# A transformer block's attention groups with their steps written in another order

## The reference

```python
x = L0_attn_u
xn = _layernorm(x, axis=-1)
x = x + _L0_attn_ref(xn, ...) + _L0_ffn_ref(xn, ...)      # state-space convolution; gated FFN
xn = _layernorm(x, axis=-1)
x = x + _L1_attn_ref(xn, ...) + _L1_ffn_ref(xn, ...)      # attention; base + gated low-rank experts
```

```python
H, DN, DV, DQ, HID = 32, 128, 128, 192, 512
q = jnp.einsum('bsd,de->bse', hidden_states, wq).reshape(B, S, H, DQ)
k, v = ...                                                # from wkv, heads of 128
scores = jnp.einsum('bqhd,bkhd->bhqk', q[..., :DN], k) * scale
scores = jnp.where(causal[None, None], scores, NEG_INF)
probs = jax.nn.softmax(scores, axis=-1)
attn = jnp.einsum('bhqk,bkhd->bqhd', probs, v).reshape(B, S, H * DV)
return jnp.einsum('bse,ed->bsd', attn, wo)
```

## Time and profile before

| | |
|---|---|
| Median of 3 runs (lowest, highest) | 1063.7 us (1060.49, 1066.61) |
| The profiled execution: its own time | 1062.6 us |
| Its span, first to last instruction | 1060.7 us |
| Granted TensorE clock | 1.000 of full speed over the whole span |
| Layer 0, up to the first step of group 0 | 0 to 263 us |
| Group 0, groups 1 to 6, group 7 | 263 to 353, 353 to 960, 960 to 1061 us |
| Busy: PE, ACT, SP's DMAs | 1047.7, 543.0, 31.5% of 16 engines |

### The profile page before, as it was taken

One profiled execution on the slowest core, in us unless ns is written; L12 is line 12 of the kernel. 1 busy time (PEld: TensorE's weight loads), 2 busy tenths in 40 slices (PEclk: granted clock), 3 DMA queues, 4 the chain that ended last, 5 costly groups with the idle time before them and its releaser, 6 DMA issues. The chain is left out here.

```text
span 1060.7 us, 19733 instructions
## 1 busy us (share of the span) xinstructions
PE 1047.7 (99%) x6025; PEld 918.1 (87%) x6025; DVE 808.9 (76%) x1959; ACT 543.0 (51%) x1573; POOL 754.8 (71%) x1030
## 2 busy tenths in 40 slices
PE   9999999999999999999999999999999999999998
PEld 8888878898898898878988898889888888888987
DVE  7598974467688687877888787878788778778775
ACT  4454321033764555556555555555556555555663
POOL 4777568897957875977597668848774876587920
PEclk9999999999999999999999999999999999999999
DMA  5111242110232333334333423342434333333412
GB/s 168 51 49 52 97 143 70 60 46 21 76 99 82 115 115 99 98 102 132 80 97 118 133 82 96 104 135 75 126 86 123 87 113 111 105 92 109 119 55 79
DMA packets 108120, 100.67 MB, mean 95 GB/s; under 512 B 72688, under 2 KB 88240, under 8 KB 107888
## 3 DMA queue, kind: packets, MB, share of 16 engines
q1 hardware_dynamic: 107728, 98.89, 31.5%
q10 hardware_dynamic: 288, 0.52, 0.1%
HBM read 74.26 MB, written 25.10 MB: 94 GB/s over the span
## 5 line engine op out<-in xcount | busy, mean ns | idle before, releaser
L2063 ACT ACTIVATE prob<-prob,top 128x128 f32<-128x128 f32 (+1 forms) x256 | 114.2, 448 | 85.2 <-DVE top L2096 84.6
L1724 POOL TENSOR_TENSOR form_lo<-wqk_stage,form_hi 128x256 fp32r<-128x256 f32 x192 | 143.5, 748 | 16.0
L2069 ACT ACTIVATE prob<-prob,inv 128x128 f32<-128x128 f32 (+1 forms) x256 | 102.8, 450 | 51.1 <-DVE inv L2102 51.1
L1778 POOL TENSOR_SCALAR vf_hi<-wvo_stage 128x512 fp32r<-128x512 f32 (+1 forms) x48 | 26.6, 554 | 117.4 <-PE banks L200 85.2
L198 PE MATMUL banks<-tT_hi,form_hi 128*128 128x512 f32 x256 | 103.7, 405 | 0.8 <-DVE qT_lo L1851 0.5
L199 PE MATMUL banks<-tT_lo,form_hi 128*128 128x512 f32 x256 | 100.0, 391 | 0.0
L200 PE MATMUL banks<-tT_hi,form_lo 128*128 128x512 f32 x256 | 100.0, 391 | 0.0
L2096 DVE CUSTOM_DVE_ANT_0 prob<-banks,mask 128x128 f32<-128x128 f32 (+1 forms) x256 | 81.0, 353 | 23.0 <-issue 7.6
L2114 DVE TENSOR_TENSOR acc<-acc,banks 128x512 f32<-128x512 f32 x129 | 86.4, 675 | 15.5 <-PE banks L200 14.3
L198 PE MATMUL banks<-wo_hi,oT_hi 128*128 128x512 f32 x240 | 97.1, 404 | 0.7 <-DVE oT_lo L2133 0.7
L199 PE MATMUL banks<-wo_lo,oT_hi 128*128 128x512 f32 x240 | 93.8, 391 | 0.0
(11 more groups left out here) (358 smaller groups left out, 3638.9 us busy)
## 6 DMA issues: line engine op xcount, KB each, us to landing
bounce<-probT SPq DMA_DIRECT2D x117, 192.0 KB, 1.9
pT<-bounce SPq DMA_DIRECT2D x468, 48.0 KB, 1.9
wqk_stage<-in_w_qk SPq DMA_DIRECT2D x32, 512.0 KB, 4.0
wvo_stage<-in_w_v SPq DMA_DIRECT2D x34, 256.0 KB, 3.2
wvo_stage<-in_w_o SPq DMA_DIRECT2D x32, 256.0 KB, 2.9
wd_stage<-in_w_down SPq DMA_DIRECT2D x22, 256.0 KB, 2.6
gu_stage<-in_w_gu SPq DMA_DIRECT2D x10, 512.0 KB, 3.5
out<-acc SPq DMA_DIRECT2D x7, 256.0 KB, 2.0
```

The source lines that it names most:

```text
L1724: nc.gpsimd.tensor_tensor(form_lo[:, part], src[:, :], as_f32(form_hi[:, part]), ALU.subtract).then_inc(form_ready, 1)
L2063: ins = nc.scalar.activation(pr, pr, ACT.Exp, bias=top[:, n % 2, r:r + 1], scale=-1.0, accum_out=total[:, n % 2, r:r + 1])
L2069: ins = nc.scalar.activation(pr, pr, ACT.Copy, scale=inv[:, n % 2, r:r + 1])
```

## The change

The three lists are written anew. Each keeps its steps, and each step what it does; only the order differs: output products stand behind other steps of a slot, adds of the output units (W) are spread over slots, and loads (D, K), transposes (Z) and halves (L, M, H) shift with them. No function is changed; POOL's order is the same.

```diff
--- before.py
+++ after.py
@@ -82,59 +82,58 @@
 
 
 FIRST = listed("""
-    S0 X0 R0 D0 D1 Z0
-    S1 X1 L0.5 P0.3 P1.1 L0.3 P1.6 R1 P1.2
-    S2 H0 Q0.1 T1 X2 L1.2 P1.7 O0 U1 R2 P1.4
-    S3 O1 T2 L1.4 U2 E1 X3 K2 R3 D2 D3 P1.5 Q0.6 Q0.2
-    S4 O2 T3 U3 L1.5 X4 R4 M0.2 Q0.7 K3 P1.3
-    S5 O3 E3 T4 U4 X5 R5 P2.1 L1.3 P2.6 O4
-    S6 T5 U5 X6 R6 Q0.4 P2.2 D4 O5 Z6
-    S7 M0.4 K4 L2.2 D5 E5 P2.7 X7 R7 P2.4 Z7 L2.4 P2.5 W1.0
-    S8 H6 L2.5 W1.1 X8 R8 P2.3 O6 Z8
-    S9 L2.3 X9 R9 Q0.5 M0.5 Z9 W1.2 P3.1 H7 Q0.3 M0.3 Q1.1
-    S10 O7 H8 E7 X10 R10 Q1.6 Q1.2 M1.2 Z10
-    S11 K5 P3.6 P3.2 O8 H9 Q1.7 X11 R11 L3.2 Q1.4 Z11 P3.7 M1.4 P3.4 L3.4 W1.3 W1.4 O9 H10 E9
-    S12 X12 Q1.5 R12 P3.5 M1.5 Z12 L3.5
-    S13 X13 O10 W1.5 Q1.3 M1.3 H11 R13 P3.3 W1.6 D6 Z13 L3.3 O11 W1.7 E11
-    S14 H12 D7 X14 R14 Z14 P4.1 P4.6 P4.2
-    S15 L4.2 O12 H13 X15 P4.7 R15 P4.4 L4.4 Z15 O13 E13 P4.5
+    S0 X0 L0.5 R0 D0 D1 Z0
+    S1 P0.3 L0.3 X1 P1.1 R1 K2 P1.6 P1.2 Q0.1 L1.2
+    S2 H0 T1 X2 P1.7 O0 U1 R2 P1.4 O1
+    S3 T2 L1.4 U2 X3 E1 R3 P1.5 D2 D3 Q0.6 Q0.2
+    S4 L1.5 O2 T3 U3 X4 R4 M0.2 Q0.7 P1.3 O3
+    S5 E3 T4 U4 X5 P2.1 R5 L1.3 K3 P2.6 D4 O4
+    S6 T5 U5 X6 R6 Q0.4 P2.2 Z6 M0.4 D5 K4 O5
+    S7 E5 X7 L2.2 P2.7 R7 P2.4 L2.4 Z7 W1.0 P2.5
+    S8 H6 X8 L2.5 R8 P2.3 W1.1 W1.2 Z8 L2.3
+    S9 X9 Q0.5 O6 R9 P3.1 M0.5 H7 Q0.3 Q1.1 Z9
+    S10 O7 E7 M0.3 Q1.6 H8 X10 R10 Q1.2 P3.6 K5 Z10
+    S11 X11 P3.2 M1.2 O8 H9 R11 Q1.7 L3.2 P3.7 Q1.4 Z11 P3.4 O9 L3.4 M1.4 W1.3 W1.4 E9 H10
+    S12 X12 Q1.5 R12 P3.5 M1.5 Z12
+    S13 X13 L3.5 W1.5 O10 R13 Q1.3 W1.6 M1.3 H11 P3.3 P4.1 Z13 L3.3 O11 D6 W1.7
+    S14 D7 E11 H12 P4.6 X14 R14 P4.2 O12 Z14
+    S15 H13 X15 L4.2 P4.7 R15 P4.4 L4.4 Z15 O13 E13 P4.5
 """)
 MIDDLE = listed("""
-    D0
-    S0 H-2 D1 X0 K2 L0.5 P0.3 P1.1 R0 Z0
-    S1 X1 W0.0 W0.1 O-2 H-1 L0.3 R1 P1.6 P1.2 W0.2 O-1 Z1
-    S2 X2 L1.2 H0 E-1 R2 P1.7 P1.4 W0.3 Z2
-    S3 X3 L1.4 W0.4 O0 H1 W0.5 R3 D2 W0.6 P1.5 Z3 Q0.1
-    S4 O1 L1.5 H2 X4 R4 Z4 K3 E1 P1.3 P2.1 Q0.6
-    S5 W0.7 O2 H3 X5 L1.3 Q0.2 D3 R5 M0.2 Q0.7 D4 Z5
-    S6 O3 H4 E3 X6 R6 Q0.4 P2.6 P2.2 Z6 K4 M0.4 O4
-    S7 L2.2 P2.7 H5 D5 X7 P2.4 O5 R7 L2.4 E5 H6 P2.5 Z7
-    S8 X8 L2.5 R8 P2.3 L2.3 Z8
-    S9 X9 O6 W1.0 P3.1 H7 Q0.5 W1.1 R9 M0.5 Q0.3 W1.2 Z9
-    S10 O7 E7 H8 Q1.1 X10 R10 M0.3 Q1.6 Z10 Q1.2 M1.2
-    S11 X11 P3.6 K5 Q1.7 Q1.4 R11 P3.2 M1.4 Z11 L3.2 O8 P3.7 H9 P3.4 Q1.5 W1.3 L3.4 W1.4 O9
-    S12 H10 E9 X12 R12 P3.5 W1.5 M1.5 O10 Z12 L3.5 W1.6 H11
-    S13 X13 Q1.3 M1.3 R13 D6 D7 P3.3 Z13 L3.3 P4.1 O11 W1.7 E11
-    S14 H12 X14 R14 P4.6 P4.2 Z14 O12
-    S15 L4.2 P4.7 H13 X15 R15 P4.4 L4.4 Z15 O13 E13 P4.5
+    S0 X0 D0 D1 H-2 R0 L0.5 P0.3 P1.1 Z0
+    S1 X1 W0.0 L0.3 O-2 H-1 K2 P1.6 R1 P1.2 Z1 W0.1
+    S2 O-1 W0.2 L1.2 E-1 W0.3 H0 X2 R2 Z2 P1.7 P1.4
+    S3 W0.4 X3 O0 L1.4 H1 Q0.1 R3 D2 P1.5 Z3 W0.5
+    S4 K3 O1 E1 W0.6 H2 X4 R4 L1.5 Z4 P1.3 P2.1 W0.7 L1.3
+    S5 D3 X5 R5 Q0.6 O2 Z5
+    S6 H3 Q0.2 M0.2 Q0.7 O3 H4 E3 D4 X6 R6 Q0.4 P2.6 Z6 P2.2 O4
+    S7 M0.4 L2.2 P2.7 H5 X7 R7 P2.4 L2.4 Z7 O5 E5 K4 H6 P2.5
+    S8 L2.5 X8 R8 P2.3 Z8 P3.1 O6 W1.0
+    S9 X9 D5 L2.3 Q0.5 H7 P3.6 W1.1 R9 M0.5 Q0.3 Q1.1 Z9
+    S10 O7 H8 M0.3 Q1.6 X10 R10 Z10 Q1.2 M1.2
+    S11 E7 Q1.7 K5 W1.2 X11 R11 P3.2 Q1.4 M1.4 Z11 L3.2 W1.3 P3.7 O8 H9 P3.4 Q1.5 L3.4 O9 M1.5 W1.4
+    S12 E9 H10 X12 R12 P3.5 Z12
+    S13 L3.5 X13 Q1.3 W1.5 R13 D6 O10 W1.6 H11 M1.3 P3.3 P4.1 Z13 L3.3 W1.7 O11 E11
+    S14 H12 P4.6 X14 R14 D7 P4.2 O12 Z14
+    S15 L4.2 P4.7 H13 X15 R15 P4.4 Z15 L4.4 O13 E13 P4.5
 """)
 LAST = listed("""
-    S0 L0.5 H-2 X0 R0 P0.3 D0 D1 Z0 P1.1 L0.3 P1.6
-    S1 O-2 H-1 W0.0 W0.1 X1 R1 Z1 W0.2 W0.3 O-1 E-1 H0 P1.2
-    S2 X2 L1.2 P1.7 R2 K2 P1.4 Z2 O0
-    S3 H1 L1.4 W0.4 W0.5 X3 R3 Z3 W0.6
-    S4 P1.5 L1.5 O1 E1 H2 D2 K3 D3 X4 P1.3 Q0.1 R4 W0.7 O2 L1.3 Z4 H3
-    S5 X5 Q0.6 Q0.2 R5 P2.1 Z5 M0.2 Q0.3 M0.3
-    S6 O3 E3 H4 X6 R6 P2.6 P2.2 Z6
-    S7 D4 O4 L2.2 H5 X7 P2.7 R7 P2.4 Z7 L2.4 D5 O5 Q1.1 Q1.6 E5
-    S8 H6 X8 Q1.2 R8 P2.5 Z8 M1.2
-    S9 O6 H7 X9 L2.5 R9 P2.3 Z9 P3.1 Q1.3 L2.3 M1.3 O7 E7 H8 P3.6 P3.2
-    S10 L3.2 P3.7 X10 R10 P3.4 O8
-    S11 T10 L3.4 H9 X11 R11 P3.5 O9 W1.0 U10 E9 W1.1
-    S12 L3.5 T11 X12 O10 U11 R12 P3.3 L3.3 W1.2 O11
-    S13 T12 E11 U12 X13 R13 W1.3 W1.4 O12
-    S14 T13 U13 W1.5 X14 R14 W1.6 O13 E13
-    S15 T14 W1.7 U14 X15 R15 W2.0 W2.1 O14 T15 U15 W2.2 O15 E15 W2.3 W2.4 W2.5 W2.6
+    S0 L0.5 H-2 X0 R0 P0.3 D0 D1 W0.0 Z0 P1.1 L0.3 P1.6
+    S1 O-2 H-1 W0.1 X1 R1 Z1
+    S2 O-1 K2 E-1 P1.2 W0.2 W0.3 H0 L1.2 P1.7 X2 R2 Z2 P1.4
+    S3 D2 O0 W0.4 H1 L1.4 K3 X3 R3 W0.5 W0.6 Z3
+    S4 P1.5 L1.5 O1 H2 X4 Q0.1 R4 Z4 E1 P1.3 P2.1 D3
+    S5 W0.7 O2 H3 L1.3 X5 R5 Q0.6 Q0.2 Z5
+    S6 X6 M0.2 Q0.3 O3 H4 E3 R6 M0.3 P2.6 P2.2 Z6
+    S7 O4 H5 L2.2 X7 R7 P2.7 P2.4 Q1.1 Z7 L2.4 O5 Q1.6 D4 E5 D5
+    S8 H6 X8 R8 P2.5 Z8 Q1.2
+    S9 O6 L2.5 H7 X9 P2.3 M1.2 R9 P3.1 L2.3 Z9 Q1.3 P3.6
+    S10 M1.3 O7 E7 H8 P3.2 L3.2 P3.7 X10 R10 P3.4
+    S11 O8 H9 L3.4 T10 X11 R11 P3.5 O9 E9 U10 W1.0 W1.1 W1.2
+    S12 T11 O10 U11 X12 R12 L3.5 P3.3 O11
+    S13 T12 U12 E11 L3.3 X13 R13 W1.3 W1.4
+    S14 O12 T13 U13 X14 W1.5 R14 O13 E13
+    S15 W1.6 T14 U14 X15 W1.7 R15 W2.0 W2.1 T15 O14 U15 W2.2 O15 E15 W2.3 W2.4 W2.5 W2.6
 """)
 LAST = LAST + [
     ("W", 2, NT - 1, slice(0, HALF_D)), ("W", 2, NT - 1, slice(HALF_D, DM))]
```

## The result

The changed kernel takes 1054.7 us (median of 6 runs, 1054.25 to 1055.4). The kernel before, on the same chip, takes 1062.3 us (6 runs, 1060.49 to 1066.61). The ratio is 0.9924, 95% interval 0.9905 to 0.9942: faster by 0.76%. The profiled execution took 1054.9 us around a span of 1053.2 us; before it was 1062.6 around 1060.7.

A forecast was written before the change was run, and what follows sets the result against it. PE, busy 1047.7 of 1060.7 us, bounds the kernel, so only its 14.8 us of waits can go. They fall to 8.7 (minus 6.1), plus 1.4 unlisted: net minus 4.7 from the 1063.7 median, 1059.0 us, range 1052 to 1066.

The forecast's parts named there:

- bare group of 99 us: A middle group without PE's waits takes 99.05 us, and the new order leaves that unchanged.
- O-2 and O-1: Start of a group: H-2 behind X0 uses up the cover, so waits rise from 0.8 to 3.6 us.
- O13: End of a middle group: Q1.4 later puts POOL's wo_lo behind H13; waits fall from 4.85 to 1.5 us.
- O5: Output product of pair 5: Z5 further ahead, DMA no longer last; waits fall from 3.3 to 1.2 us.
- P1.4, W0.4, P0.3: Z15 ahead of L4.4 and E-1 ahead of H0 remove waits in middle groups: 3.5 to 0.6 us.
- Small waits: Small waits over the six middle groups, new close pairs included: 0.6 us stays 0.6, bound 2.
- The two close pairs that I named: P2.4 behind M0.4 and S14 behind L3.3: distances of 2.5 and 2.7 us instead of 3.9 and 4.1.
- such unlisted ones: Close places not listed among the steps of a group: 0.23 us a group added, 1.4 us in all.
- First and last group: Waits at the program's ends: 0.6 us in the first group; in the last, O9 goes from 0.7 to 0.
- A: Rival: nearly all waits go because O-2 and O-1 stay in time; minus 12, 1051.7 us; chance 0.17.
- B: Rival: no net change, H13 again meets a 1.29 us POOL instruction; 1062.4 us; chance 0.17 with sums like it.
- C: Rival: slower, H-2 behind X0 makes O-2 and O-1 wait, price 12.6 us; 1068.0 us; chance 0.11.

The follow-up runs named there:

- a2: The changed kernel with H-2 moved further back in MIDDLE, behind R0 and L0.5: 1058.6 us, ratio 0.9963 to the kernel before.
- e1: The kernel before with the new MIDDLE list alone, FIRST and LAST staying old: 1055.8 us, ratio 0.9931.
- e3: The kernel before with two swaps in MIDDLE, Z15 ahead of L4.4 and E-1 ahead of H0: 1060.6 us, ratio 0.9974.
- a5: The changed kernel with Q1.4 back ahead of R11 and P3.2 in MIDDLE: 1057.1 us, ratio 0.9937 to the kernel before.
- a6: The changed kernel with the load D7 back ahead of Z13 in MIDDLE, SP's order alone: 1063.9 us, ratio 1.0001 to the kernel before.
- e4: The kernel before with only the loads K3, D3 and D4 moved in MIDDLE to where the changed kernel has them: 1062.3 us, ratio 0.9994.
- e2: The kernel before with one edit in MIDDLE, Q1.4 behind R11 and P3.2: 1069.4 us, ratio 1.0062.
- e5: The kernel before with Q1.4 behind P3.2, W1.3 ahead of O8 and D7 behind Z14: 1063.2 us, ratio 1.0007.
- a7: The changed kernel with M0.4 ahead of O4 and S7, and H13 ahead of P4.7, in MIDDLE: 1053.8 us, ratio 0.9906 to the kernel before.

## Why the prediction came out as it did

The forecast was 1059.0 us with a range of 1052 to 1066; the time is 1054.7. The direction and the place of the gain (waits alone, with a bare group of 99 us) were right, and most mechanisms; one term was badly sized, and another came out well in part by luck. 599.3 us of the middle less its 5.2 us of waits is 594.1 us, 99.0 a group, where I had 99.05. The sum of waits was 3.8 us too high. Beyond that, the kernel before, timed again beside the changed one, took 1.4 us less than the median that I started from, and the 0.7 us behind the last matmul went the other way.

- *O-2 and O-1: the mis-sized term.* I had 3.6 us and it is 0. The cover was read rightly as nearly nothing, and a2 shows that past it each tenth is paid. What failed is the step "With X0 first, H-2 on ScalarE comes at about 458.85 and on VectorE at 459.25 to 459.7", with "or as much in the new frame". I let X0 start where H-2 had started, 3.33 us behind S0, and H-2 4.33 behind. But X0 starts 2.86 behind S0 (555.99) and H-2 3.74. The cause is VectorE, which fills S0's row tiles for X0: it reaches them 1.98 us behind PE, and in group 2 of before 2.45 us (the timeline has 456.97 there). I took its backlog at the group's start as unchanged; it shrinks by 0.47 us. The stretch by POOL, for which I charged 0.4 us, did come: VectorE's part of H-2 took 0.89 instead of 0.42 us. On my start (4.73 us behind S0) that is an end at 5.62, 0.4 us late, as I charged; on the real start (4.18) it is 5.07, in time. e1's group 1, with VectorE 2.73 us behind and H-2 at 0.85, has the wait of 0.43 that I forecast for each group. That Z15's swap, which takes away the wait of 1.03 us ahead of L4.4, is what shortened the backlog is argued: e3, with the swap, has less cost at O-1 (0.09 instead of 0.88), but no run took the swap out of the changed kernel.
- *O13: right in size, right in mechanism, with two conditions missing.* a5 undoes the move of Q1.4 alone and O13 returns to 4.74 us with H13 at 1.19: what POOL runs beside H13 sets this wait, and Q1.4 sets what POOL runs. But my step named S13 and O11 and not D7. With POOL later, SP's wait for it in front of D7 holds the bounce of pair 13 longer. a6 shows 6.96 us, above my upper bound of 4.85. The Trainium skill ("DMA: Bandwidth & Descriptors", section "Anatomy of one DMA — SWDGE (gpsimd) path") says that DMA engines never wait on semaphores, the issuing sequencer does before it sends a transfer off. The section is about the path that GpSimd feeds, but SP's rows in a6 agree with it. That D7 moves behind Z13 is as necessary as Q1.4, and W1.3 between L3.2 and P3.4 (6.3 us without it) the third. My costing of Q1.4's shift looked at POOL and not at the ring that the swap reorders. Neither D7 nor W1.3 was in my reasoning, and the new order had moved both: that O13 came out near my figure is luck to that extent.
- *O5: right.* 1.2 forecast, 0.59 measured; H5 lies near the edge in group 1 alone (0.45), and ScalarE's part of it never waits for the DMA now. What I missed is why groups 1 and 4 to 6 paid before and 2 and 3 did not: SP's long issues.
- *P1.4, W0.4, P0.3: right.* 0.6 forecast, 0.27 measured. e3 shows the swap for W0.4 by itself; for P1.4 no run parts the swap from the long issue that is gone too. I read group 2's late loads as the work of Z15 alone, and the long issue of 2.07 us, which I did not see in the rows, had the larger share. The forecast did not hang on it: loads 1.35 us sooner and P1.4 wanted 1.37 us later are more than the 0.62 and 0.76 us that groups 1 and 2 paid. Nor does the wait need a long issue: e4's group 2 pays 0.56 without one.
- *Small waits: too low.* The two close pairs that I named cost 1.02 (P2.4, 0.17 a group) and, at S14, nothing. P2.3's cost grew from 0.43 to 1.18, a place that I did not list. I had added 0.23 us a group for such unlisted ones; it is about that size (1.18 less 0.43, and T12's 0.24, are 1.0 against 1.4).
- *First and last group: right.* O9 fell from 0.70 to 0.08, W2.4 stays at 0.38.
- *Rivals.* The outcome lies between the forecast and A (6.3 us of waits against 10.1 and 2.8). A's sum was wrong: by its own words (3.6 and 1.4 become 0.8, O13's 1.5 and O5's 1.2 halve, 0.6 stays four times) 4.6 us are left, which gives 1053.5 us and not 1051.7. So summed, A is 1.2 us from the measured time and the forecast 4.3. B did not come: H13 takes 0.76 us, and a5 shows what its case costs, 2.6 us. C did not come; a2 is a mild form of it and costs 3.8 us.

In the kernel before, the changed one and a5 the trace has H13 ending 0.28 us behind POOL's instruction in every middle group, whether that instruction takes 0.75 or 1.29 us; in e2's groups 1 to 3 POOL's is the one that is lengthened. The Trainium skill ("SBUF — State Buffer", section "Who interferes with whom") says that VectorE and GpSimd share a port pair under an exclusive lock, that a VectorE instruction with two inputs in SBUF contends for it with a GpSimd instruction that reads SBUF, and that the order of issue decides which of the two blocks. These traces agree.

## What to carry to other kernels

Where one engine is 99% busy, price each wait at its place and ask for every moved step four things: which bank it now takes and who releases it, which engine's phase it shifts, what that engine's instruction will lie beside, and what an in-order DMA queue holds back behind a transfer that waits for that engine. Look for waits that only some of equal groups have: what differs there is not the order. Test a gain by undoing single parts of the finished order, not only by doing single parts of it in the old one: one edit (Q1.4) made the old order 6 us slower and, undone in the new one, costs 2.3. And measure cover from the moment at which the engine could start, not from where it started before.

## What the runs showed of the hardware

- POOL's copies lengthen VectorE's subtraction as well as its subtractions do. In e5, group 3, H13 took 0.90 us beside wo_hi, which has one input, and both began at 652.50. Where both begin within 0.01 us either can be the one that is lengthened: in e2's groups 1 to 3 H13 took 0.42 us and wo_lo 1.56 to 1.57 instead of 1.29.
- The same bounce through DRAM (pair 5), out to the issue of its way back, takes 1.9 to 2.3 us when the last load left 1.1 to 2.5 us ahead of it (e4, six groups), 3.15 to 3.3 us when a load of 256 KB left 0.53 us ahead (the changed kernel) and 2.8 to 4.0 us behind three loads, the last 0.9 to 1.8 us ahead (before).
- SP's issue of a transfer takes 0.43 us as a rule; all 120 issues of 1.1 us or more in the fourteen traces overlap a packet of the instruction queue. Where one falls just ahead of data that PE needs, the wait is larger (O5 in before: 0.41 to 1.32 us in the four groups with one, 0.02 and 0.09 in the two without).
- The add and the stores behind the last matmul ended the program 2.6 us behind PE in twelve of the fourteen profiled kernels, and 3.3 and 3.4 us in the changed kernel and a7, whose last instructions are the same: there the last store took 2.40 and 2.55 us to land instead of 1.71.
